# Splitting the attention weights one unit later at the start of a gated attention and expert kernel

## What is computed

```
x = x + tanh(g_xattn) * attention(layernorm(x), ctx, Wq, Wk, Wv, Wo, q_norm_w, k_norm_w, pos, itok)
x = x + tanh(g_ffn)   * experts(layernorm(x), w_router, w_gate, w_up, w_down, ws_gate, ws_up, ws_down)
```

```
q = (draft @ Wq.T)                 # 16 heads of 128
kv_in = concatenate([context, draft], axis=1)
k = (kv_in @ Wk.T); v = (kv_in @ Wv.T)   # 4 heads of 128
q = rope(rms_norm(q, q_norm_w)); k = rope(rms_norm(k, k_norm_w))
attn = softmax(q k^T / sqrt(128)) v      # 4 query heads share a key head
return attn @ Wo.T
```

## Time and profile before

| what | value |
|---|---|
| median of 3 runs | 1235.36 us (1235.15 to 1236.42) |
| profiled execution, its own time | 1235.88 us |
| its span from the first to the last instruction | 1234.1 us |
| PE busy | 1198.6 us (97%) |
| DVE, ACT, POOL busy | 1015.6, 885.7, 925.6 us |
| mean granted TensorE clock | 0.993 |

### The profile page before, as it was taken

One profiled execution on the slowest core, in us unless ns is written; L12 is line 12 of the kernel. 1 busy time (PEld: TensorE's weight loads), 2 busy tenths in 40 slices (PEclk: granted clock), 3 DMA queues, 4 the chain that ended last, 5 costly groups with the idle time before them and its releaser, 6 DMA issues.

```text
span 1234.1 us, 31450 instructions
## 1 busy us (share of the span) xinstructions
PE 1198.6 (97%) x8773; PEld 1137.1 (92%) x8774; DVE 1015.6 (82%) x3003; ACT 885.7 (72%) x3756; POOL 925.6 (75%) x1118
## 2 busy tenths in 40 slices
PE   3799999999999999999999999999999999999998
PEld 1599999999999999999999999999999899999997
DVE  8899888888888888888888888888888677777443
ACT  8887777777777777777777777777777546666322
POOL 3688888888888888888888888788887526556654
PEclk8999999999999999999999999999999999999999
DMA  6624333332222232223333333322236536555574
GB/s 177 199 91 129 93 98 104 110 93 89 89 89 89 89 94 89 94 89 93 97 112 109 99 99 111 114 76 75 75 109 183 211 103 188 164 165 152 184 235 155
DMA packets 128788, 148.50 MB, mean 120 GB/s; under 512 B 13824, under 2 KB 108288, under 8 KB 127968
## 3 DMA queue, kind: packets, MB, share of 16 engines
q1 hardware_dynamic: 122256, 130.16, 35.1%
q0 software_dynamic: 6480, 17.77, 3.9%
HBM read 66.93 MB, written 80.76 MB: 120 GB/s over the span
## 4 chain that ended last, share of the span: by engine, by line
PE 94%; DVE 3%; ACT 2%; issue 1%; POOL 0%; DMA 0%; SPq 0%; DVEq 0%; POOLq 0%
PE b_kv L1681 14%; PE b_o L1762 14%; PE b_q L1667 14%; PE b_sc L1736 9%; PE b_aT L1751 9%; PE b_pT L1744 5%; PE b_qT L1725 4%; PE b_q L1980 3%; PE b_kv L1980 3%; PE b_kT L1721 2%; PE b_q L1777 2%; PE b_kT L1777 2%; PE b_aT L1895 1%; PE b_aT L1997 1%; PE b_pT L1997 1%; PE b_kT L1869 1%
## 5 line engine op out<-in xcount | busy, mean ns | idle before, releaser
L1681 PE MATMUL b_kv<-w_group,kv_in_hi 128*128 128x256 f32 x992 | 205.5, 305 | 0.2 <-DVE k_sin L1233 0.2
L731 POOL TENSOR_TENSOR qk_r<-qk_me,minus_half 128x6 f32<-128x6 f32 x128 | 174.2, 1361 | 10.0
L941 ACT ACTIVATE probs<-b_sc,neg_max 128x128 f32<-128x128 f32 x512 | 180.0, 371 | 0.3 <-DVE neg_max L1257 0.3
L735 POOL TENSOR_TENSOR q_rot<-q_rot,q_sin 128x512 f32<-128x512 f32 x128 | 165.2, 1290 | 7.1 <-DVE q_sin L1247 2.2
L1681 PEld LDWEIGHTS b_kv<-w_group,kv_in_hi 128*128 128x128 f32 x992 | 162.0, 190 | 7.0 <-issue 0.8
L1667 PE MATMUL b_q<-w_group,kv_in_hi 128*128 128x512 f32 x496 | 165.0, 414 | 0.0
L935 ACT ACTIVATE pT<-b_pT 128x512 f32<-128x512 f32 x128 | 76.6, 598 | 103.8 <-PE b_pT L1744 101.9
L1762 PE MATMUL b_o<-wo_hi,aT_hi 128*128 128x256 f32 x496 | 148.5, 299 | 0.2
L738 POOL TENSOR_TENSOR q_rot<-q_rot,qk_r 128x512 f32<-128x512 f32 x128 | 133.6, 1043 | 10.0
L1736 PE MATMUL b_sc<-kT,qT 128*128 128x128 f32 x1024 | 136.0, 276 | 4.0 <-ACT qT L930 3.9
L1681 PE MATMUL b_kv<-w_group,kv_in_lo 128*128 128x256 f32 x496 | 139.8, 282 | 0.0
(11 more groups left out here) (292 smaller groups left out, 3939.1 us busy)
## 6 DMA issues: line engine op xcount, KB each, us to landing
xs_scratch<-zeros SPq DMA_DIRECT2D x34, 1032.0 KB, 6.4
s_in<-xs_scratch SPq DMA_DIRECT2D x71, 129.0 KB
yT_scratch<-yT SPq DMA_DIRECT2D x32, 256.0 KB, 2.0
yS<-yT_scratch SPq DMA_DIRECT2D x32, 256.0 KB, 3.5
routed<-ys_scratch SPq DMA_DIRECT2D x32, 256.0 KB, 3.6
w_hi_all<-w_scratch SPq DMA_DIRECT2D x3, 1536.0 KB, 13.0
x_in<-in_x SPq DMA_DIRECT2D x32, 128.0 KB, 2.3
ctx_raw<-in_ctxT SPq DMA_DIRECT2D x32, 128.0 KB, 2.6
```

The source lines that it names most:

```text
L731: nc.gpsimd.tensor_tensor(qk_r[g % 2][:], qk_me[:], minus_half[:, 0:REP + NB], ALU.pow).then_inc(r_ready, 1)
L735: nc.gpsimd.tensor_tensor(q_rot[g % 2][:], q_rot[g % 2][:], q_sin[g % 2][:], ALU.add) \
L941: last = nc.scalar.activation(probs[:, j, :], b_sc[:, j * P:(j + 1) * P], ACT.Exp, bias=neg_max[g % 2][:, j:j + 1], accum_out=row_sum[g % ...
L1681: last = nc.tensor.matmul(b_kv[:, s * 2 * HD:(s + 1) * 2 * HD], kv_in[p][a][:, c, 2 * s:2 * s + 2, :], wkv_of(b, c)[:, g % KVH, :], start= ...
```

## The change

In the first pair alone the order of some steps on ACT and DVE is another, and one wait of PE.

- ACT: the splits of pieces 0 and 1 leave unit 0 for unit 1 (0 before `normed_hi`, 1 behind the exponentials), pieces 2 and 3 leave unit 1 for unit 2, 4 and 5 unit 2 for unit 3, 6 and 7 unit 3 for unit 4, 8 goes to unit 5, 9 and 10 stand in unit 6, 11 in unit 7. `queries_out(1)` stood at the end of unit 0, ahead of `query_squares(2)`; it now stands at its usual place in unit 1.
- DVE: pieces 0 and 1 move from the middle of unit 1 to its end, 2 and 3 to the end of unit 2, 4 and 5 to that of unit 3, 6 and 7 to that of unit 4, 8 and 9 to the ends of units 5 and 6; in unit 7 piece 10 stands behind `score_max` and piece 11 behind `top_two`. `context_lo(1, 1)` moves behind `turn_keys` and `normed_lo`.
- PE: the wait for `w_lo` of 12 stood ahead of `keys_values` in unit 7, and now stands behind it.

```diff
--- before.py
+++ after.py
@@ -1024,18 +1024,19 @@
                         key_squares(n + 1, g + 1)
                     if first and u == 0:
                         act.wait_ge(st_trig_first, 16 * 2)
-                    if not (first and u == 1):
-                        queries_out(n, g)
+                    queries_out(n, g)
                     if not (end and g == 3):
                         values_out(n + 1, g + 1)
                     if not (first and u == 0):
                         normalize_first(n - 1, g - 1)
                     if g == 2 and part is not None:
                         piece_hi(t, i, p, part)
+                    if first and u == 1:
+                        split_hi(pieces[0:1])
                     if first and 2 <= u < 5:
-                        split_hi(pieces[2 * u:2 * u + 2])
-                    if first and 5 <= u < 7:
-                        split_hi(pieces[5 + u:6 + u])
+                        split_hi(pieces[2 * u - 2:2 * u])
+                    if first and 5 <= u < 8:
+                        split_hi(pieces[{5: slice(8, 9), 6: slice(9, 11), 7: slice(11, 12)}[u]])
                     if g == 0 and not end:
                         context_hi(t + 1, i + p, 1 - p)
                     if g == 1 and not end:
@@ -1048,11 +1049,9 @@
                         tables(X0 + 3)
                         exponent_table()
                     exponentials(n, g)
-                    if first and u < 2:
-                        split_hi(pieces[2 * u:2 * u + 2])
-                    if first and u == 0:
-                        queries_out(1, 1)
-                    else:
+                    if first and u == 1:
+                        split_hi(pieces[1:2])
+                    if not (first and u == 0):
                         attended_hi(n - 1, g - 1)
                     if not (end and g >= 2):
                         query_squares(n + 2, g)
@@ -1450,18 +1449,15 @@
                         residual(t - 1, i - 1 + p, 1 - p)
                     if g == 2 and not first:
                         normalize_y(t - 1, 1 - p)
+                    score_max(n, g)
                     if first and u == 7:
-                        split_lo(pieces[11:12])
-                    score_max(n, g)
+                        split_lo(pieces[10:11])
                     if g == 1 and not (first and p == 0):
                         layer_stats2(t - 1, 1 - p)
                         need(dve, stats2, t)
                     if g == 3 and not last:
                         layer_stats(t + 2, i + 1, p)
                         need(dve, stats_done, t + 3)
-                    if first and u == 1:
-                        split_lo(pieces[0:2])
-                        context_lo(1, 1)
                     if not (end and g == 3):
                         turn_keys(n + 1, g + 1, p1)
                     if g == 0 and not first:
@@ -1470,6 +1466,8 @@
                         copy_logits(t - 1)
                     if g == 1 and not end:
                         normed_lo(t + 1, 1 - p)
+                    if first and u == 1:
+                        context_lo(1, 1)
                     if g == 2 and not (first and p == 0):
                         tokens_lo(t - 1, 1 - p)
                     if end and g == 3:
@@ -1488,7 +1486,7 @@
                         keys_out(1, 1)
                         normalize_x(1, 1)
                     if first and 0 < u < 7:
-                        split_lo(pieces[2 * u:2 * u + 2] if u < 4 else pieces[4 + u:5 + u])
+                        split_lo(pieces[2 * u - 2:2 * u] if u < 5 else pieces[3 + u:4 + u])
                     if g == 0 and not first:
                         rows_of_tokens(t - 2, p)
                     if g == 0 and not (end or first and p == 0):
@@ -1497,6 +1495,8 @@
                         layer_var2()
                     if g == 3 and not (first and p == 0):
                         top_two(t - 1)
+                    if first and u == 7:
+                        split_lo(pieces[11:12])
                     if g == 3 and not last:
                         layer_var(p)
                     if g == 2 and part is not None:
@@ -1846,12 +1846,12 @@
                         attend(n - 1, g - 1)
                     if first and 2 <= u < 6:
                         pe.wait_ge(w_lo, 2 * (u - 2) + 2)
-                    if first and u == 7:
-                        pe.wait_ge(w_lo, SPLITS + 4)
                     if first and u < 2:
                         first_keys_values(u + 2)
                     elif not (end and g >= 2):
                         keys_values(n + 2, g + 2, t2, p2)
+                    if first and u == 7:
+                        pe.wait_ge(w_lo, SPLITS + 4)
 
 
             def tokens_T(t, p):
```

## The result

The changed kernel takes 1237.76 us (median of 21 runs, 1237.00 to 1238.38), the kernel before 1235.75 us beside it (21 runs, 1234.77 to 1236.94). The ratio is 1.0015, with a 95% interval of 1.0009 to 1.0021: slower by 1.9 us (1.1 to 2.6).

The account below looks back on a forecast made before the run. The prediction took TensorE (PE), busy 97% of the span, to bound the kernel; −3.7 us at the front and +4.25 us at the back gave +0.55 us, a median of 1235.9 us, range 1233.4 to 1238.4.

Parts of the forecast that it names:

- front: two holes: Units 0 to 2: PE's idles of 0.77 and 2.53 us close, a gain taken as 3.7 us.
- ninth split: Ahead of unit 6's `project`: PE waits for this split, which ends later on DVE, costing 0.45 us (0 to 0.7).
- tenth split: Ahead of unit 7's `project`: PE waits for this split, now ending with DVE's unit 6, costing 0.9 us (0.3 to 1.15).
- keys: Unit 7: a split ahead of the turned keys now follows the score maximum, beside POOL's `query_sum`, costing 0.5 us (0 to 0.75).
- twelfth split: End of unit 7: PE waits ahead of unit 8's transposes for this split, now last behind `top_two`, costing 1.8 us.
- loop entry: End of unit 7: PE's branch into its loop no longer lies under products, costing 0.3 us (0 to 1.5).
- second rival: End of unit 7: PE fetches the loop's code only after the wait, 3.5 us; +3.75 in all, 1239.1 us; chance 0.12.
- Half of it meets slack in unit 5: DVE's unit 4 gets 0.6 us more work; part is absorbed, so PE waits only 0.3 us (0 to 0.65).
- from 110 us on every row is within 1 us of before's: Sign that the forecast is right: past 110 us the new trace's rows lie within 1 us of the old.
- The first rival: Units 2 to 9: DVE catches up, so most of the front's gain stays; −2.6 us, 1232.8; chance 0.12.
- The third: Rival near 48 us: late table stores hold ACT at `attended_hi(0)`, some 1.3 us; +1.85 in all, 1237.2 us; chance 0.06.

Follow-up runs that it names:

- a_again: The changed kernel unaltered, timed and profiled a second time; ratio 1.0016 against the kernel before.
- a_fourth: The changed kernel unaltered, run again for its profile alone; units 1 to 12 sum to 95.46 us, against 94.06 in the kernel before.
- e3_act_only: The kernel before with only ACT's new order in units 0 and 1, DVE's splits left in place; ratio 0.9992 against the kernel before.
- e4_both_early: The changed kernel with DVE's twelfth split directly behind the eleventh in unit 7, ahead of unit 8's turned keys; ratio 1.0008 against the kernel before.
- e5_wait_ahead: The changed kernel with PE's wait for 12 splits put back ahead of `keys_values` in unit 7; ratio 1.0033 against the kernel before.
- e7_ctx_only: The kernel before with only DVE's context low part moved behind unit 2's turned keys, splits left in place; ratio 0.9992 against the kernel before.
- e8_front_orders: The kernel before with ACT's new order and the context low part moved, DVE's splits left in place; ratio 0.9982 against the kernel before.

## Why the prediction was right and wrong

By its steps, in unit times; "at full clock" is the mean of a_again and a_fourth.

| step of the prediction | forecast | at full clock | with the low clock |
|---|---|---|---|
| front: two holes (units 1 to 4) | -3.7 | -4.2 | -4.1 |
| unit 5 | +0.3 | +0.7 | +0.7 |
| unit 6, ninth split | +0.45 | +0.8 | +0.8 |
| unit 7: tenth split, keys, twelfth split, loop entry | +3.5 | +3.5 | +3.5 |
| unit 8 | 0 | +0.1 | +1.7 |
| unit 9 | 0 | +0.6 | +0.2 |
| sum to unit 12 | +0.55 | +1.4 | +2.7 |

- **The front** came as forecast: `qk_me` 2.3 us earlier in a_again, which starts like before (forecast 2.2), both holes closed. The 0.4 us above the 3.7 are in units 3 and 4, which I had taken as equal.
- **Unit 7** is right in its sum and mixed within it: the tenth split 0.56 (0.9), `keys_values` 0.92 with 0.23 of it there before, so 0.69 (0.5), the twelfth split and the entry 1.98 (1.8 + 0.3), and some 0.3 by the same reckoning outside those waits. The entry, from the split's end to PE's start, is 0.35 us; the second rival, 3.5 us for it, is excluded, and with it a fetch of the kind that the Trainium skill describes in "Runtime: NRT & Kernel Launch", section "Instruction fetch mechanics", at a size that counts here: the trace shows 0.35 us at most for it.
- **Units 5 and 6 were mis-sized**: "Half of it meets slack in unit 5" fails. DVE's timeline has no idle from 69.70 to 81.90 us, so nothing took up the piece of 0.6 us put into its unit 4, and PE lost 0.7. PE waited 0.66 us for the ninth split, not 0.45. A part of unit 5's 0.7 is again a row beside POOL: the context's low part stood beside `cos_w`, and took 1.22 us in the changed kernel and 0.41 in before, where `cos_w` met another row (`x_n`, 0.95 us instead of 0.40). What each of the two is worth wasn't tried apart. The rows, the first two of the changed kernel, the last of before:

```profile
72.55 1.22 DVE L1213 TENSOR_TENSOR kv_in_lo<-ctx_raw,kv_in_hi 128x256 fp32r<-128x256 f32 x1
...
72.41 1.07 POOL L710 TENSOR_TENSOR cos_w<-trig_raw,w_cos 128x384 f32<-128x384 f32 x1
...
76.45 0.41 DVE L1214 TENSOR_TENSOR kv_in_lo<-ctx_raw,kv_in_hi 128x256 fp32r<-128x256 f32 x1
```

- **Two terms were missing.** I had written that behind about 110 us nothing changes, and had priced each stall by its own length. A stall has an aftermath: the engines come out of it shifted against each other, which put a DVE product beside `cos_w` in unit 9 (+0.6); and in two of four profiles the granted clock fell to 0.5 behind the stall (some +1.25 net). The mean of the two, 2.05 us, less the forecast of 0.55 leaves 1.5: 0.6 by the clock, 0.7 by units 8 and 9 at full clock, and 0.7 in units 5 and 6, less 0.5 that the front gave more. So the sign "from 110 us on every row is within 1 us of before's" failed, at +1.4 and +2.7, and that the time stayed within 0.2% owes something to luck: without the front's extra 0.5 us the mean would be 2.55.
- **The first rival** (the back doesn't pay) fell, and the argument against it held: DVE still waited 0.74 us for ACT's exponentials ahead of 69.70, so it could not run ahead. **The third** didn't come: no idle stands before ACT's `aT_first` at 47.46. SP waited 11.1 us for the twelfth split (4.4 before) and issued the tables of tile 3 from 99.22 on; POOL's `cos_w` started at 106.81 directly behind its own work, so those loads cost 0, as forecast.

## What to carry to other kernels

Work that is moved off one wait on a full engine comes back as a wait wherever that engine next sets the pace; count the idle of that engine unit by unit before you call half of it slack. Moving only the order (ACT's squares and the context part) gave 2.2 us for nothing, moving the splits in pairs one unit back turned that to a loss, and spreading them in ones and twos with the last wait at its use gave 2.8 (the two gains are not told apart: 1.1 to 3.3 and 1.7 to 4.1). Price a stall with what follows it, the engines' shift against each other and the clock, and look at several profiles of one kernel before you believe a stretch of low clock.

## What the runs showed of the hardware

Between 45 and 110 us, a granted clock of 0.50 appears in five of the fourteen profiles of this study, and each time with an idle of TensorE of 1.86 us or more just ahead of it (1.86 in e3_act_only, 1.98 and 1.97 in two profiles of the changed kernel, 2.06 in e4_both_early, 4.29 in e5_wait_ahead). It begins within some 1.5 us behind the idle's end, in e5 inside the idle, and stays for 3 to 4 us, in e5 for nearly 7. Three profiles show such an idle and no fall: 2.53 us in before, 1.97 us in a_again and in a_fourth. Idles of 1.34 us (e7_ctx_only) and 1.61 us (e8_front_orders) had none. Ahead of 45 us, nine profiles, before's among them, have an idle of 2.43 to 3.11 us up to about 35 us and a granted clock of 0.50 for some 3 us between 36 and 41 us; the other five, the form of 8.75 us, have an idle of 1.55 to 1.83 us there and no fall. What decides is open; it wasn't tried apart.

In the first profile of the changed kernel the `wo_lo` split took 1.19, 1.31, 1.83 and 1.21 us at its four places (79.99, 87.94, 92.50, 97.99). The two longer ones started while a product of POOL ran (86.84 to 88.17 and 92.21 to 93.25), the two shorter ones while POOL stood idle. `probs` times `row_inv` took 0.61 us in before and 1.38 in a_again at the same place in unit 8. So the length of such a DVE row depends on what POOL does beside it as well as on its shape. Not every overlap costs: the split at 46.13 in before took 1.22 us, though it started inside a POOL row of 128x6 elements (`qk_r`, 45.33 to 46.65).
